# A three-phase graph network on one core: how many message slots TensorE picks and how many GpSimd gathers, in the first two phases

## What is computed

```python
def mean_aggregate(x, src, dst, num_nodes):
    msgs = x[src]
    summed = jax.ops.segment_sum(msgs, dst, num_segments=num_nodes)
    deg = jax.ops.segment_sum(jnp.ones((src.shape[0],), x.dtype), dst, num_segments=num_nodes)
    return summed / jnp.maximum(deg, 1.0)[:, None]

h = x @ W_lin + b_lin
agg1 = mean_aggregate(h, src, dst, N)                 # first pick phase sums this (16 columns, after W1_agg)
h = jnp.tanh(agg1 @ W1_agg + h @ W1_root + b1)
agg2 = mean_aggregate(h, src, dst, N)                 # second pick phase
x = layernorm(x + jnp.tanh(agg2 @ W2_agg + h @ W2_root + b2))
...
h_src = (x @ Wn.T + bn)[src]                          # third phase: gated messages
agg = jax.ops.segment_sum(h_src * w, dst, num_segments=N)
```

## Time and profile before

| what | us |
|---|---|
| median of 3 runs | 8763.74 |
| the profiled execution | 8762.05 |
| its span, first to last instruction | 8760.1 |
| TensorE matmul busy | 7637.1 (87%) |
| GpSimd busy | 6259.5 (71%) |
| ScalarE busy | 5860.1 (67%) |
| VectorE busy | 5505.1 (63%) |

### The profile page before, as it was taken

How to read it: one execution, slowest core, us unless ns; L and a number is a source line. 1 busy time by engine, 2 the same in 40 slices (tenths; PEclk the granted TensorE clock), 3 DMA queues, 4 the chain that set the end, 5 groups by cost and what they waited for, 6 DMA issues and landing times. The chain is left out here.

```text
span 8760.1 us, 165117 instructions
## 1 busy us (share of the span) xinstructions
PE 7637.1 (87%) x51516; PEld 6905.6 (79%) x51517; DVE 5505.1 (63%) x7447; ACT 5860.1 (67%) x10176; POOL 6259.5 (71%) x6471
## 2 busy tenths in 40 slices
PE   7999999999989999999999777777777777888887
PEld 6999999888889999998888666666666666776775
DVE  5655656666645555556666666666666666777777
ACT  5777777666657777776666566666666666666665
POOL 5777777766557777777664477777777777777776
PEclk9999999999989999999999798988988889999999
DMA  2111112111111111111111222222222222222222
GB/s 75 35 34 35 35 34 35 31 30 28 25 40 34 35 34 35 34 34 31 31 30 23 75 56 59 55 57 57 55 58 56 55 59 55 55 59 56 55 56 59
DMA packets 341135, 392.62 MB, mean 45 GB/s; under 512 B 165119, under 2 KB 240563, under 8 KB 340564
## 3 DMA queue, kind: packets, MB, share of 16 engines
q0 software_dynamic: 204000, 151.96, 12.1%
q1 hardware_dynamic: 136750, 239.87, 8.1%
q10 hardware_dynamic: 322, 0.03, 0.0%
HBM read 375.47 MB, written 15.92 MB: 45 GB/s over the span
## 5 line engine op out<-in xcount | busy, mean ns | idle before, releaser
L699 PE MATMUL banks<-split_sb,e_low_hot 128*128 128x400 f32 x22000 | 4092.6, 346 | 45.6 <-DVE split_sb L752 45.6
L699 PEld LDWEIGHTS banks<-split_sb,e_low_hot 128*128 128x128 f32 x22000 | 4015.6, 189 | 74.1 <-DVE split_sb L752 46.1
L922 POOL DMA_INDIRECT big<-hn_table,src_i x2875 | 2857.0, 994 | 883.7 <-issue 870.7
L645 POOL DMA_INDIRECT big<-p_table,src_i x1750 | 1655.8, 946 | 695.2 <-issue 528.7
L758 DVE TENSOR_REDUCE picked<-banks 128x48 f32<-128x1200 f32 x1000 | 1300.1, 1300 | 1352.1 <-PE banks L699 1351.1
L670 ACT ACTIVATE e_low_hot<-e_key_off 128x1536 fp32r<-128x1536 f16 x1000 | 1381.1, 1381 | 1130.6 <-PE banks L699 1112.7
L645 POOL DMA_INDIRECT big<-h_table,src_i x1750 | 1674.9, 957 | 612.5 <-issue 529.6
L666 ACT ACTIVATE e_key_off<-e_key_in,node_off 128x384 f16<-128x384 f16 (+1 forms) x4000 | 2028.4, 577 | 125.5 <-DMA e_key_in<-sel_dram 41.4
L957 PE MATMUL banks<-hn_split,e_low_hot 128*128 128x448 f32 x7000 | 1500.1, 370 | 75.5 <-issue 70.1
L957 PEld LDWEIGHTS banks<-hn_split,e_low_hot 128*128 128x128 f32 x7000 | 1298.0, 188 | 217.1 <-issue 96.6
L781 DVE TENSOR_TENSOR hot<-e_dst_pair,banks 128x1536 bf16<-128x1536 bf16 (+1 forms) x934 | 931.1, 997 | 69.9 <-issue 0.6
(11 more groups left out here) (216 smaller groups left out, 4491.7 us busy)
## 6 DMA issues: line engine op xcount, KB each, us to landing
e_wide<-in_edge_t SPq DMA_DIRECT2D x125, 832.0 KB
e_key_in<-sel_dram SPq DMA_DIRECT2D x250, 343.8 KB
big<-hn_table,src_i POOLq DMA_INDIRECT x2875
big<-p_table,src_i POOLq DMA_INDIRECT x1750
big<-h_table,src_i POOLq DMA_INDIRECT x1750
e_key_in<-gate_dram SPq DMA_DIRECT2D x125, 64.0 KB
src_i<-in_src SPq DMA_DIRECT2D x375, 12.5 KB, 1.7
e_key_in<-sel_dram SPq DMA_DIRECT2D x250, 8.2 KB
```

The source lines that it names most:

```text
L645: pool.indirect_dma_start(buf[u][:, j, 0:ROW0], None, table, bass.IndirectOffsetOnAxis(ap=src_i[u][:, j:j + 1], axis=0),).then_inc(gathere ...
L699: last = pe.matmul(o, low_hot[gr][:, h, e], split_sb[:, part, h * HI1:(h + 1) * HI1, :], start=(h == 0 and part == 0), stop=(h == HI2 - 1 ...
L922: pool.indirect_dma_start(buf[u][:, j, 0:F], None, table, bass.IndirectOffsetOnAxis(ap=src_i[u][:, j:j + 1], axis=0),).then_inc(gathered[u ...
```

## The change

The sizes of the groups of picks become a table by the block's place in its turn of four, and for the last four blocks a row of its own. In both pick phases a block n with n % 4 == 3, up to block 119, has groups of 3, 3, 2, 2 (ten picks, fifteen gathers) and blocks 121 to 124 have 2, 2, 2, 2 (eight picks, seventeen gathers). All others stay at eleven and fourteen. The picks are the last slots of a block, as before. The thresholds of `gathered` follow. All four low_hot tiles have room for three picks, so groups of two are written and read with a gap. The order of the work on every engine is as before.

```diff
-SIZE = (3, 3, 3, 2)
-SEL = sum(SIZE)
-NGR = len(SIZE)
-AT = (0, 3, 6, 9)
+SIZE = ((3, 3, 3, 2), (3, 3, 3, 2), (3, 3, 3, 2), (3, 3, 2, 2))
+TAIL_SIZE = (2, 2, 2, 2)
+SEL = max(sum(s) for s in SIZE)
+NGR = len(TAIL_SIZE)
+MOST = max(max(s) for s in SIZE)
...
-            took = SLOTS - SEL
-            low_hot = [tiles.enter_context(nc.sbuf_tensor(f"{tag}_low_hot{gr}", [P, HI2, SIZE[gr] * P], F32R))
+            turns = (NB - 3) // bufs
+            tail = bufs * turns + 1
+
+            def sizes(n, u):
+
+                return TAIL_SIZE if isinstance(n, int) and n >= tail else SIZE[u % bufs]
+
+            def at(size, gr):
+
+                return SEL - sum(size) + sum(size[0:gr])
+
+            def gathers(n, g, u):
+
+                return 16 * sum(SLOTS - sum(sizes(m, u)) for m in range(bufs * turns + u % bufs, n + 1, bufs)) + \
+                    16 * (SLOTS - sum(SIZE[u])) * turns if isinstance(n, int) and n >= bufs * turns else \
+                    16 * (SLOTS - sum(SIZE[u])) * (g + 1)
+
+            low_hot = [tiles.enter_context(nc.sbuf_tensor(f"{tag}_low_hot{gr}", [P, HI2, MOST * P], F32R))
                        for gr in range(NGR)]
...
-                            sp.wait_ge(gathered[u], 16 * took * (g + 1))
+                            sp.wait_ge(gathered[u], gathers(n, g, u))
...
-                        for j in range(took):
+                        for j in range(SLOTS - sum(sizes(n, u))):
...
-                    def low_hots(gr, n, turn, u):
-                        es = slice(AT[gr] * P, (AT[gr] + SIZE[gr]) * P)
-                        off = key_off[:, :, 0:SIZE[gr] * P]
+                    def low_hots(gr, n, turn, u, size):
+                        es = slice(at(size, gr) * P, (at(size, gr) + size[gr]) * P)
+                        off = key_off[:, :, 0:size[gr] * P]
...
-                        act.activation(low_hot[gr][:, :, :], off, ACT.Relu, bias=1.0,
+                        act.activation(low_hot[gr][:, :, 0:size[gr] * P], off, ACT.Relu, bias=1.0,
...
-                        for k in range(SIZE[gr]):
+                        for k in range(sizes(n, u)[gr]):
...
-                        pe.wait_ge(gathered[u], 16 * took * (g + 1))
+                        pe.wait_ge(gathered[u], gathers(n, g, u))
...
-                    def take(gr, n):
+                    def take(gr, n, size):
...
-                        dve.tensor_reduce(picked[:, AT[gr]:AT[gr] + SIZE[gr], :], found, AX.X,
+                        dve.tensor_reduce(picked[:, at(size, gr):at(size, gr) + size[gr], :], found, AX.X,
...
-                    def parts(u):
-                        o = buf[u][:, SLOTS - SEL:, :]
+                    def parts(u, size):
+                        s = at(size, 0)
+                        o = buf[u][:, SLOTS - sum(size):, :]
...
-                        dve.memset(buf[u][:, SLOTS - SEL:, ONES:LO], 1.0)
+                        dve.memset(buf[u][:, SLOTS - sum(SIZE[u]):, ONES:LO], 1.0)
```

More of the change, by code:

```diff
@@ L674, in body @@
                         for gr in range(NGR):
-                            low_hots(gr, n, turn_of(g, u), u % 2)
+                            low_hots(gr, n, turn_of(g, u), u % 2, sizes(n, u))
                     for u in range(bufs):
@@ L689, in _, with pick @@
                     pe.sem_inc(hot_used[1], 1)
-                    def pick(gr, n):
+                    def pick(gr, n, u):
                         pe.wait_ge(low_made, NGR * n + gr + 1)
                         pe.wait_ge(pick_taken, NGR * n + gr + 1)
-                        for k in range(SIZE[gr]):
+                        for k in range(sizes(n, u)[gr]):
                             e = slice(k * P, (k + 1) * P)
@@ L722, in body @@
                         if inside(n + 1):
-                            pick(0, n + 1)
+                            pick(0, n + 1, u + 1)
                         add_up(n, g, u)
                         if inside(n + 1):
-                            pick(1, n + 1)
-                            pick(2, n + 1)
-                            pick(3, n + 1)
+                            for gr in range(1, NGR):
+                                pick(gr, n + 1, u + 1)
                     pe.wait_ge(split_made, 4)
                     for gr in range(NGR):
-                        pick(gr, 0)
+                        pick(gr, 0, 0)
                     with pe.Fori(0, turns) as g:
@@ L752, in split_table @@
                             dve.tensor_tensor(rests[:, at], full_in[h], top, ALU.subtract).then_inc(split_made, 1)
[L754 removed]
+                    def take(gr, n, size):
                         dve.wait_ge(pick_psum, NGR * n + gr + 1)
[L756 removed]
+                        found = banks[:, BANK0[gr] * 512:(BANK0[gr] + size[gr]) * 512].rearrange(
                             "p (s c) -> p s c", c=512)[:, :, 0:PICK].rearrange("p s (a f) -> p s f a", f=H)
[L758 removed]
+                        dve.tensor_reduce(picked[:, at(size, gr):at(size, gr) + size[gr], :], found, AX.X,
                                           ALU.max).then_inc(pick_taken, 1)
[L761 to L762 removed]
+                    def parts(u, size):
+                        s = at(size, 0)
+                        o = buf[u][:, SLOTS - sum(size):, :]
                         dve.drain()
[L764 removed]
+                        dve.tensor_copy(o[:, :, HI:HI + H], picked[:, s:, :])
                         dve.drain()
[L766 removed]
+                        dve.tensor_tensor(rest[:, s:, :], picked[:, s:, :], o[:, :, HI:HI + H], ALU.subtract)
                         dve.drain()
[L768 removed]
+                        dve.tensor_copy(o[:, :, MID:MID + H], rest[:, s:, :])
                         dve.drain()
[L770 removed]
+                        dve.tensor_tensor(o[:, :, LO:LO + H], rest[:, s:, :], o[:, :, MID:MID + H],
                                           ALU.subtract).then_inc(msgs_made, 1)
@@ L789, in body @@
                         make_hot(0, n, 0, since + 1)
-                        take(3, n)
-                        parts(u)
+                        take(3, n, sizes(n, u))
+                        parts(u, sizes(n, u))
                         with dve.Fori(since, to) as visit:
@@ L808, in body @@
                             for gr in range(3):
-                                take(gr, n + 1)
+                                take(gr, n + 1, sizes(n + 1, u + 1))
                     dve.tensor_copy(iota_ps, iota_half[:, :].bitcast(F32))
@@ L817, in _ @@
                     for gr in range(3):
-                        take(gr, 0)
+                        take(gr, 0, SIZE[0])
                     with dve.Fori(0, turns) as g:
```

3 lines of the change are left out of this document (1 added, 2 removed).

## The result

The changed kernel takes 8779.91 us (median of 20 runs, 8770.2 to 8791.81), the kernel before 8764.31 us (20 runs beside them). The ratio is 1.0016 with a 95% interval of 1.0009 to 1.0022: 8 to 19 us slower. The forecast was 8740 us (8722 to 8758), faster. The change made the kernel a little slower instead.

A forecast was written before the change was run, and what follows sets the result against it. TensorE sets the pace while GpSimd lives on its head start, then GpSimd's gathers bind. First phase -15.2 us, second -6.3, together -21.5 (clock's +2.5 included) from 8762.05: 8740 us, range 8722 to 8758.

The forecast's parts named there:

- GpSimd's lead: Blocks 0 to 78: gathers' head start over TensorE's adds shrinks 3.3 (3.9) us per four blocks, ending near blocks 27 and 20.
- The pitch: Time from one gather to the next, both pick phases: stays at 1.2507 us in the first, 1.2617 in the second.
- The add of block 78: First add of block 78, gathers setting the pace: near 1487 and 3905 us, so +12.6 and +24.0 us.
- the tail: Last four blocks: twelve picks, 17.6 us, less 3.0 us of VectorE stall: -14.5 us a phase; GpSimd's lead covers the gathers.
- TensorE's gain per pick: Both pick phases: each removed pick of eight matmuls saves 1.46 us of TensorE; 84 picks, 123 us.
- the two-window stretch: Blocks 79 to 120: TensorE leads, ten blocks 83 to 119 each give 1.46 us back: -14.6 us a phase.
- TensorE account: After block 78: wrong if a ten-pick block gives less than 1.4 us of its pick's 1.46.
- The clock: 1.2 GHz level around block 78 after TensorE's waits for gathers: +2.5 us in the first phase, nothing more in the second.
- VectorE's chain: Two-window blocks: adds wait for VectorE's hot half; if it binds at once, 21 us lost, 8761 us; 17 in 100.
- The gathers did not slow down: Answers the rival of slower gathers in both pick phases: each 0.01 us of pitch costs 22.5 us; 9 in 100.
- held for a hot build of 1.02 us: VectorE two-port mode holds each of 38 gathers on the path: 39 us, 8779; 1 of the slower-gather rival's 9 in 100.
- the two-window blocks don't give their pick back: Rival for blocks after 78: half of 2 x 14.6 us and another 2 x 3 us go, 8761 us; 17 in 100.

The follow-up runs named there:

- e5b_early: Against the kernel before: ten picks in every fourth block of blocks 0 to 79 alone, eleven elsewhere; ratio 1.0030, 26 us slower.
- with the filling: Small constant matmuls where TensorE waits, blocks 80 to 124; against the kernel before 0.9980 (eleven picks), 0.9954 (the changed kernel's picks), 0.9848 (ten in blocks 80 to 119).
- e4c_none: Control against the kernel before: eleven picks everywhere, loops cut in two, wider low_hot tiles; ratio 1.0000.
- e3b_late: Against the kernel before: eleven picks to block 79, ten in every fourth to 119, eight in the last four; ratio 0.9973, 24 us faster.
- e6_late_all: Against the kernel before: ten picks in every block 80 to 119, eight in the last four, no small matmuls; ratio 0.9923, 68 us faster.
- e7_after_fill: The changed kernel's picks plus small constant matmuls in TensorE's waits, blocks 80 to 124; ratio 0.9954 against the kernel before, 40 us faster.
- e11b_best: Against the kernel before: ten picks in blocks 80 to 122, nine and eight in the last two, small constant matmuls; 8614.5 us, ratio 0.9829.

## Why the prediction was wrong

**GpSimd's lead: right.** The pitch held. The lead was forecast to end near blocks 27 and 20; it was down to the 1.9 us of landing at blocks 25 and 20. The first "block used" wait came at blocks 102 and 103 (forecast about 102). The add of block 78 was forecast at 1487 and 3905 and came at 1487.6 and 3902.5. The second match is partly luck: 3905 is the time before plus 24.0, without the 15.2 us that the forecast itself took off the first phase. Counted from block 0's first add, block 78's came 14.5 and 25.2 us later than before (forecast 12.6 and 24.0). The last gather ended 42 and 43 us ahead of the last block's adds, not 36, so the tail did not run out of lead. e5b_early shows the account by itself: the single-window tens only cost.

**TensorE's gain per pick: right in its own terms.** The single block saved its 1.46 us (14.80 us for 80 matmuls), and with the clock held both the two-window stretch and the tail gave the forecast within 1.3 us a phase. In the changed kernel as it stands a ten-pick block of the two-window stretch gave only 0.6 us (12.6 us over twenty), under the 1.4 that the prediction had named as the sign that its TensorE account is wrong. The price of a pick was right; what failed is the next term.

**The clock: the step that failed.** "I charge the first phase ... +2.5 us; the second paid it already" took a fall of the clock for an event of one place, where TensorE had waited for a gather, and put the clock at nothing in the forty blocks behind it and in the tail. The kernel before already had 34.1 and 20.5 us at 1.2 GHz in its two-window stretches, with a pause in every block there. I had read that wait (kernel before, waits 1500 to 2350 us: 41 times, up to 1.5 us) and not asked what shorter blocks between the same pauses would do:

```profile
PE banks L717 <- DVE acc L805: 49.3, 41, 1.5
```

Time at 1.2 GHz in that stretch, one number for each phase of each profile:

| picks in blocks 80 to 119 | at 1.2 GHz, us | with the filling |
|---|---|---|
| eleven | 17.1, 20.5, 23.9, 23.9, 34.1, 58.0 | 0, 0 |
| ten in every fourth | 44.4, 47.8, 54.6, 61.4 | 0, 0 |
| ten in all | 99.0, 116.0 | 0, 0 |

(In this order: e4c_none's second phase, before's second, e4c_none's first and e5b_early's first, before's first, e5b_early's second; the changed kernel and e3b_late; e6_late_all.)

Against the filled kernels of the same picks a microsecond at 1.2 GHz costs 0.30 to 0.48 us of the stretch, in ten of the twelve 0.39 or more, as (833.3 - 812.1) / 44.4 = 0.48. The mean goes from 29.6 to 52.1 us with one pick in forty-four gone, which takes back some 10 of the 14.6 us of each phase. The spread is wide, and one stretch of eleven picks (58.0) lies above the changed kernel's own two, so the size is sure only as a mean. The tail is the same in small: 23.1 and 24.8 us at 1.2 GHz where there were 8.6 and 8.7. The profiled pair fell short of the forecast by 16.6 us in the two-window stretches and by 12.6 us in the tails. So the clock term was not +2.5 but near 30 us, and it used up the forecast gain of 24. The rest of the profiled pair's +11 us is the +4.3 behind the second phase and 1.6 in the single-window stretches; no profile shows where the medians lose their other 5 us (+16).

The Trainium skill (TensorE: Matmul & The Clock Gate, section "A second HAM failure mode: psum-queue depth-cycling") tells of a kernel in which frequent short idle times between groups of matmuls make the clock switch back and forth between its two levels, at a cost in throughput. By that, pauses of up to 1.5 us in every two-window block were a warning. The runs agree: 17.1 to 116.0 us at 1.2 GHz a stretch with the pauses, none with them filled.

**The rivals.** VectorE's chain did not bind in the two-window stretch (e7_after_fill). The gathers did not slow down: median 945 and 956 ns, and none was held for a hot build of 1.02 us (the longest, 1696 ns, lies 0.74 us above its median). None of the priced rivals was what happened. A rival "the two-window blocks don't give their pick back" stood there, with 21 us, but for another reason than the one that acted.

## What to carry to other kernels

A picture of who waits for whom prices an instruction at the clock of the rows it was read from. Before taking work off TensorE, look at the granted clock of the stretch: where it is already under 1.00 with short pauses in each block, shorter blocks between the same pauses can run more of their time at 1.2 GHz, as here, and the pauses, not the matmuls, are what to fill first. Here matmuls of a constant, done while TensorE waits anyway, gave 0.20% by themselves and 1.7% together with the picks that they made worth removing (ten picks in every late block gave 0.8% without them). And an engine that is busy 71% can have no time left: multiply the pitch, issue included, by the count, and follow its lead from block to block.

## What the hardware showed that I had not expected

- The same blocks of eleven picks spend quite different times at 1.2 GHz: 17.1 to 58.0 us of a stretch, and the stretch took 837.0 and 854.1 us. (The 58.0 us are e5b_early's, whose blocks before that stretch were changed; its other phase, changed in the same way, had 23.9, so whether that matters is open.) In a single profile that looks like an effect of an edit.
- Seventeen 128x128 matmuls of a constant in a 20 us block, 1.3 us of busy time that adds nothing to the result, made all of it disappear, in eight stretches out of eight (e11b_best's two with them).
- Two kinds of chips: 8.76 ms and 12.5 to 12.7 ms for one kernel, and a version that is 1.7% faster on the one is 0.5% slower on the other. What sets them apart is open.
